# Counting pass of a graph kernel: a block's sums in one PSUM bank, the count as a column of each part, fewer vector operations

## What is computed

```python
h = jnp.maximum(_layernorm(x, axis=-1), 0.0)
x = x + _L1_gnn_ref(h, edge_index, L1_gnn_weight, L1_gnn_bias)

def _L1_gnn_ref(vertices, edges, weight, bias):
    ...
    agg = jax.ops.segment_sum(vertices[src], dst, num_segments=n_vertices)
    deg = jax.ops.segment_sum(jnp.ones_like(dst, dtype=vertices.dtype), dst, num_segments=n_vertices)
    agg = agg * (jnp.clip(deg, 1.0, None) ** (-0.5))[:, None]
    return agg @ weight.T + bias
```

## Time and profile before

| | |
|---|---|
| median of 3 runs | 6257.87 us (6255.64 to 6283.21) |
| the profiled execution's own time | 6250.27 us |
| its span | 6248.4 us |
| busy share of the span: PE, DVE, ACT, POOL | 76%, 77%, 58%, 21% |
| the counting pass in the trace | 2793.74 to 3337.51 us from the span's start |

### The profile page before, as it was taken

One profiled execution on the slowest core, in us unless ns is written; L12 is line 12 of the kernel. 1 busy time (PEld: TensorE's weight loads), 2 busy tenths in 40 slices (PEclk: granted clock), 3 DMA queues, 4 the chain that ended last, 5 costly groups with the idle time before them and its releaser, 6 DMA issues.

```text
span 6248.4 us, 250046 instructions
## 1 busy us (share of the span) xinstructions
PE 4754.4 (76%) x92226; PEld 3865.2 (62%) x92226; DVE 4828.7 (77%) x10876; ACT 3637.7 (58%) x10975; POOL 1301.5 (21%) x1884
## 2 busy tenths in 40 slices
PE   2566666663777777747775999996999997999997
PEld 1344444442666666636665999994666665666665
DVE  8999999998999999998887555556666665666665
ACT  3566666661333333336665666665777776777776
POOL 2555555553333333310000000000000000000000
PEclk7777777776778878869997999998999998999999
DMA  1000000002666666620001333332333332333332
GB/s 42 1 1 1 1 1 1 1 1 73 202 202 200 203 200 204 201 84 0 0 0 33 101 99 100 100 93 67 84 85 85 84 84 78 85 84 84 84 85 76
DMA packets 305213, 501.25 MB, mean 80 GB/s; under 512 B 76918, under 2 KB 78454, under 8 KB 305126
## 3 DMA queue, kind: packets, MB, share of 16 engines
q1 hardware_dynamic: 303782, 499.39, 27.8%
q0 software_dynamic: 576, 0.52, 0.0%
q10 hardware_dynamic: 768, 0.16, 0.0%
HBM read 408.40 MB, written 91.57 MB: 80 GB/s over the span
## 4 chain that ended last, share of the span: by engine, by line
issue 51%; DVE 25%; PE 14%; POOL 6%; DVEq 2%; DMA 1%; ACT 1%; POOLq 0%; ACTq 0%; SPq 0%
PE PS L1173 9%; DVE agg L1620 7%; POOL arena L627 5%; DVE arena L1584 5%; PE PS L1135 4%; DVE Hp L1584 3%; DVE arena L1626 2%; DVE tmp L1584 2%; PE PS L1180 1%; DVE arena L2161 0%; DVE arena L2171 0%; DVEq L1590 0%; DVE agg L2166 0%; DMA rows_h<-Hn 0%; DVE arena L1593 0%
## 5 line engine op out<-in xcount | busy, mean ns | idle before, releaser
L1584 DVE TENSOR_TENSOR arena<-iotab,arena 128x1024 bf16<-128x1024 bf16 (+6 forms) x1813 | 1760.4, 991 | 535.3 <-PE PS L1298 479.9
L910 ACT ACTIVATE arena<-PS 128x384 bf16<-128x384 f32 x2450 | 1076.9, 491 | 519.3 <-PE PS L1291 507.4
L1298 PE MATMUL PS<-arena 32*128 32x192 bf16 x41552 | 1069.7, 243 | 1.7 <-ACT arena L910 1.1
L748 ACT ACTIVATE arena<-PS,m 128x196 bf16<-128x196 f32 x1813 | 743.8, 429 | 547.1 <-POOLq L527 328.7
L1298 PEld LDWEIGHTS PS<-arena 32*128 32x128 bf16 x41552 | 806.2, 93 | 181.8 <-issue 156.5
L1135 PE MATMUL PS<-Hp,arena 128*128 128x72 bf16 (+1 forms) x14700 | 809.0, 204 | 104.8 <-DVE arena L1950 41.1
L1135 PEld LDWEIGHTS PS<-Hp,arena 128*128 128x128 bf16 x14700 | 696.8, 102 | 132.2 <-DVE arena L1950 41.3
L1291 PE MATMUL PS<-Hp,arena 128*128 128x192 bf16 (+1 forms) x4900 | 664.5, 250 | 115.8 <-DMA arena<-hots 60.0
L1023 PE MATMUL PS<-arena,tmp 128*128 128x262 bf16 x1813 | 508.9, 329 | 290.0 <-DVE tmp L1584 289.6
L891 ACT ACTIVATE arena<-PS,ewB 128x64 f32<-128x64 f32 x2450 | 534.8, 332 | 291.4 <-PE PS L1135 291.3
L1015 PE MATMUL PS<-agg,onesb 128*128 128x196 bf16 x1715 | 516.8, 303 | 202.5 <-ACT arena L748 198.1
(11 more groups left out here) (351 smaller groups left out, 7782.7 us busy)
## 6 DMA issues: line engine op xcount, KB each, us to landing
arena<-hots SPq DMA_DIRECT2D x735, 256.0 KB, 2.6
arena<-codes SPq DMA_DIRECT2D x245, 512.0 KB, 4.2
hots<-arena SPq DMA_DIRECT2D x245, 256.0 KB, 4.2
arena<-hots SPq DMA_DIRECT2D x147, 320.0 KB, 2.9
arena<-codes SPq DMA_DIRECT2D x49, 640.0 KB, 4.4
hots<-arena SPq DMA_DIRECT2D x49, 320.0 KB, 4.5
rows_h<-Hn SPq DMA_DIRECT2D x4, 1568.0 KB, 9.1
rows_l<-Y SPq DMA_DIRECT2D x1, 1764.0 KB, 10.4
```

The lines of the kernel that those rows point to most:

```text
L748: act.activation(junk[:, j % 4, :], ps[j % 4][:, 0:KEYS], ACT.Relu, bias=m256[:, 0:1], accum_out=rank[:, j:j + 1]).then_inc(k_rank, 1)
L910: act.activation(RG[g % 2][:, 2 * i:2 * i + 2, :].rearrange("p k c -> p (k c)"), ps[q % 2][:, 0:2 * RW], ACT.Copy).then_inc(r_ev, 1)
L1298: last = pe.matmul(ps[2 + q][:, b * RW:(b + 1) * RW], one_hot[32 * q:32 * q + 32, b * P:(b + 1) * P], rows_of[32 * q:32 * q + 32, :], star ...
L1584: return dve.tensor_tensor(to.rearrange("p k (n t) -> p k n t", t=4), iota_of[:, 0:n].rearrange("p (n t) -> p n t", t=4)[:, None, :, :] .t ...
```

## The change

`Hp` and the few's values get three parts of 65 columns each in this pass: 64 features and a count column, which is one in the first part and zero in the other two (`CV` = 65, `CW` = 195). All groups and the few of a block accumulate in bank 6. `evict` runs once a block, after group 1 of the next block: one reduction over the three parts of 65 columns, then one addition to the 65 columns of `agg`. The bank is given back between the two. `few` compares all three columns in one operation, from the fp32 `iota`, where there were three from the bf16 `iotab`. On DVE two more short memsets of `Hp` stand ahead of the pass, on POOL one more of the few's values.

```diff
-        CW = PARTS * DIM + 1
+        CW = PARTS * CV
...
-                mlink(pool.memset(c_W3m[:, :, 3 * DIM:CW], 1.0))
+                mlink(pool.memset(c_W3m, 0.0))
+                mlink(pool.memset(c_W3m[:, :, DIM:CV], 1.0))
...
-                    act.activation(Hp[:, ws, DIM:2 * DIM], Hn[:, ws, :], ACT.Copy).then_inc(s_h1, 1)
+                    act.activation(Hp[:, ws, v:v + DIM], Hn[:, ws, :], ACT.Copy).then_inc(s_h1, 1)
...
-                h = g // 3
-                to = ps[6 + h][:, 0:CW]
+                to = ps[6][:, 0:CW]
                 pe.wait_ge(f_whole, n + (NN + 3))
-                if g % 3 == 0:
-                    pe.wait_ge(f_accout, dx * 2 + (2 * WINDOWS + h + 1))
+                if g == 0:
+                    pe.wait_ge(f_accout, dx * 2 + (2 * WINDOWS + 2))
...
-            dve.memset(Hp[:, :, 3 * DIM:CW], 1.0)
+            for a in range(PARTS):
+                dve.memset(Hp[:, :, a * CV + DIM:(a + 1) * CV], float(a == 0))
...
-                def evict(dx, h):
-                    if h == 0:
-                        dve.wait_ge(f_scat, dx * NG + (NN + 3 + 3))
-                    else:
-                        dve.wait_ge(f_sum, dx + (WINDOWS + 1))
-                    got = ps[6 + h]
-                    flink(dve.tensor_reduce(c_part[:, 0:DIM], got[:, 0:RW].rearrange("p (a c) -> p c a", a=PARTS),
-                                            AX.X, ALU.add))
-                    to = agg[:, bass.ds(dx, 1), 0:DIM].rearrange("p w c -> p (w c)")
-                    degree = agg[:, bass.ds(dx, 1), DIM:DIM + 1].rearrange("p w c -> p (w c)")
-                    flink(dve.tensor_tensor(degree, degree, got[:, RW:CW], ALU.add))
-                    flink(dve.tensor_tensor(to, to, c_part[:, 0:DIM], ALU.add))
-                    dve.sem_inc(f_accout, 1)
+                def evict(dx):
+                    dve.wait_ge(f_sum, dx + (WINDOWS + 1))
+                    flink(dve.tensor_reduce(c_part, ps[6][:, 0:CW].rearrange("p (a c) -> p c a", a=PARTS), AX.X, ALU.add))
+                    dve.sem_inc(f_accout, 2)
+                    to = agg[:, bass.ds(dx, 1), 0:CV].rearrange("p w c -> p (w c)")
+                    flink(dve.tensor_tensor(to, to, c_part, ALU.add))
...
-                    for m in range(MC):
-                        last = dve.tensor_scalar(c_OM[:, m, :], iotab[:, 0:P],
-                                                 msrel[:, bass.ds(dx, 1), m:m + 1].rearrange("p w c -> p (w c)"), None,
-                                                 ALU.is_equal)
-                    last.then_inc(f_ohm, 1)
+                    dve.tensor_tensor(c_OM, iota[:, 0:P][:, None, :].to_broadcast((P, MC, P)),
+                                      bc(msrel[:, bass.ds(dx, 1), :].rearrange("p w c -> p (w c)"), P),
+                                      ALU.is_equal).then_inc(f_ohm, 1)
...
-                        if g == 2 and not first:
-                            evict(dx - 1, 1)
+                        if g == 1 and not first:
+                            evict(dx - 1)
                         if g == 3:
                             few(dx)
-                        if g == 5:
-                            evict(dx, 0)
```

More of the change, by code:

```diff
@@ L267, in gnn_stack @@
         c_OM = cv.take(MC * P, bf16).rearrange("p (m n) -> p m n", m=MC)
-        c_part = cv.take(WIDE)
+        CV = DIM + 1
+        c_part = cv.take(CV)
         c_Gm = cv.take(MC * DIM).rearrange("p (m c) -> p m c", m=MC)
         c_Rm = cv.take(MC * DIM).rearrange("p (m c) -> p m c", m=MC)
-        CW = PARTS * DIM + 1
+        CW = PARTS * CV
         c_W3m = cv.take(MC * CW, bf16).rearrange("p (m c) -> p m c", m=MC)
@@ L665, in _ @@
                 gather_few(c_Gm, th[1], 1)
-                mlink(pool.memset(c_W3m[:, :, 3 * DIM:CW], 1.0))
+                mlink(pool.memset(c_W3m, 0.0))
+                mlink(pool.memset(c_W3m[:, :, DIM:CV], 1.0))
                 pool.wait_ge(f_mg, 16 * 3 * MC)
-                split_few(c_Gm, c_Rm, c_W3m, DIM, DIM, 2 * DIM, 0)
+                split_few(c_Gm, c_Rm, c_W3m, DIM, CV, 2 * CV, 0)
             pool.wait_ge(s_table, 16 * 4)
@@ L714, in squares_and_roots, with parts_of_h @@
                                    scale=1.0 / DIM).then_inc(s_std, 1)
-            def parts_of_h(n):
+            def parts_of_h(n, v=DIM):
                 for h, ws in enumerate(HALVES):
                     act.wait_ge(s_h, 2 * n + h + 1)
-                    act.activation(Hp[:, ws, DIM:2 * DIM], Hn[:, ws, :], ACT.Copy).then_inc(s_h1, 1)
+                    act.activation(Hp[:, ws, v:v + DIM], Hn[:, ws, :], ACT.Copy).then_inc(s_h1, 1)
                 for h, ws in enumerate(HALVES):
                     act.wait_ge(s_hrest, 2 * n + h + 1)
-                    act.activation(Hp[:, ws, 2 * DIM:3 * DIM], tmp[:, ws, :], ACT.Copy).then_inc(s_h2, 1)
+                    act.activation(Hp[:, ws, 2 * v:2 * v + DIM], tmp[:, ws, :], ACT.Copy).then_inc(s_h2, 1)
             def copy_turned(n):
@@ L837, in _ @@
             squares_and_roots(2)
-            parts_of_h(1)
+            parts_of_h(1, CV)
             act.wait_ge(s_begin, 2)
@@ L1230, in apply @@
                         Hp[:, bass.ds(dx, 1), 0:CW].rearrange("p w c -> p (w c)")
-                    last = pe.matmul(to, AB[g % 3][:, k * P:(k + 1) * P], rhs, start=(g % 3 == 0 and k == 0),
-                                     stop=(g == 2 and k == GS[g] - 1))
+                    last = pe.matmul(to, AB[g % 3][:, k * P:(k + 1) * P], rhs, start=(g == 0 and k == 0), stop=False)
                 last.then_inc(f_scat, 1)
@@ L1425, in _, with split_h @@
             hs = [0]
-            def split_h():
+            def split_h(v=DIM):
                 n = hs[0]
@@ L1431, in split_h @@
                     dve.wait_ge(s_h1, 2 * n + h + 1)
-                    dve.tensor_tensor(tmp[:, ws, :], Hn[:, ws, :], Hp[:, ws, DIM:2 * DIM],
+                    dve.tensor_tensor(tmp[:, ws, :], Hn[:, ws, :], Hp[:, ws, v:v + DIM],
                                       ALU.subtract).then_inc(s_hrest, 1)
@@ L1435, in split_h, with norm_relu @@
                     dve.wait_ge(s_h2, 2 * n + h + 1)
-                    dve.tensor_tensor(Hp[:, ws, 0:DIM], tmp[:, ws, :], Hp[:, ws, 2 * DIM:3 * DIM],
+                    dve.tensor_tensor(Hp[:, ws, 0:DIM], tmp[:, ws, :], Hp[:, ws, 2 * v:2 * v + DIM],
                                       ALU.subtract).then_inc(s_hparts, 1)
-            def norm_relu(v):
+            def norm_relu(v, width=DIM):
                 center(v)
@@ L1443, in norm_relu @@
                                              op0=ALU.max, op1=ALU.mult).then_inc(s_h, 1)
-                split_h()
+                split_h(width)
             def copy_y(n):
@@ L2114, in _ @@
             OFS = [0]
-            for links in (5, 6, 3, 2, 2):
+            for links in (5, 2, 3, 2, 2):
                 OFS.append(OFS[-1] + links * WINDOWS)
@@ L2135, in _ @@
             link(dve.tensor_tensor(X[:, :, :], X[:, :, :], tmp[:, :, :], ALU.add))
-            norm_relu(X[:, :, :])
+            norm_relu(X[:, :, :], CV)
             dve.sem_inc(s_th, 1)
-            dve.memset(Hp[:, :, 3 * DIM:CW], 1.0)
+            for a in range(PARTS):
+                dve.memset(Hp[:, :, a * CV + DIM:(a + 1) * CV], float(a == 0))
             dve.tensor_copy(wide, Hn[:, :, :])
@@ L2188, in count_pass @@
                 with dve.Fori(1, WINDOWS) as d:
-                    at[0], at[1] = d * 6 + (ofs - 3), 0
+                    at[0], at[1] = d * 2 + (ofs - 2), 0
                     body(d, False)
-                at[0], at[1] = ofs + 6 * WINDOWS - 3, 0
-                evict(LASTW, 1)
+                at[0], at[1] = ofs + 2 * WINDOWS - 2, 0
+                evict(LASTW)
             with dve.If(runs > 1):
```

## The result

The median went from 6264.6 us (four runs of the kernel before, 6255.6 to 6283.2) to 6179.4 us (four runs, 6174.4 to 6187.2); ratio 0.986, interval 0.983 to 0.989. The profiled execution of the changed kernel took 6187.2 us with a span of 6185.2. The difference of the medians is 85 us, that of the two profiled executions 63 us; both need an account.

What follows compares the result with a forecast made beforehand. DVE was taken to set the counting pass's pace. Gains of 1.8 + 59.3 − 0.3 − 0.2 = 60.6 us took the profiled 6250.3 to 6189.7; 7.6 more for the median gave 6197 us, range 6180 to 6217.

Steps and rivals of the forecast that it cites:

- the sum: Counting pass and the memsets ahead: 1.8 + 59.3 − 0.3 − 0.2 = 60.6 us gained.
- the last step: From profiled execution to median: 6189.7 us plus 7.6, the runs' median being above the profiled execution, so 6197.
- The period: One block of the counting pass on DVE: 9.69 us, 1.29 less than 10.98.
- The low clock: Short clock drops in the counting pass: kept at their old price, 4 us; gone, they would give 4 back.
- more is gained: Rival: no low clock (4 us), a cheaper few's operation (12 us), or either: 6181 to 6193; chance 0.17.
- The ends: First and last block of the counting pass: 1.8 us gained at the start, 0.3 lost at the end.
- the loop's turn: At a block's end on DVE: 0.30 us, taken as hidden behind two comparisons without a wait between.
- the new wait: DVE ahead of the remaining evict's reduction, waiting for PE's sums: 0.63 us a block.
- the single bank: At apply(0) of the new block: bank back at 3.85 us against 3.84 before, costing PE nothing at full clock.
- the few's operation: The few's one-hots on DVE: one operation at 0.48 us against three at 0.49, so nothing gained.
- PE is just in time: PE ahead of build(0): of 1.74 us idle the removed evict takes 1.63, leaving 0.11.
- The slower rival: New waits at the single bank break up PE's bursts, the clock drops; at half the pass 6312 us; chance 0.03.

Runs made afterwards that it cites:

- e1: The changed kernel again, no edit, beside the kernel before: median 6185.1 us against 6284.7, ratio 0.983.
- e2: The changed kernel with the few's one-hots made by three operations again: 6189.0 us, ratio 0.986 to the kernel before.
- e4: The kernel before once more, no edit, a single profiled execution: counting pass 542.2 us, time 6259.0 us.
- e3: The changed kernel with the one evict behind group 2 of the next block instead of group 1: median 6173.1 us, ratio 0.981.
- e9: The changed kernel with the one evict behind group 0 instead of group 1: counting pass 559.1 us, single execution 6271.7 us.
- e11: The changed kernel plus an unread vector addition of 2176 elements in group 5, pausing PE 2.43 us: pass 621.6 us, execution 6334.9 us.
- e8: The changed kernel plus an unread vector addition of 1408 elements in group 5, pausing PE 1.62 us: counting pass 546.1 us.
- e10: The changed kernel with the one evict behind group 3 instead of group 1: counting pass 443.2 us, single execution 6145.7 us.
- e12: The changed kernel with the evict behind group 3, timed in six runs: median 6157.7 us, ratio 0.986 to the kernel before.
- e5: The changed kernel plus 167 extra unread matmuls ahead of the weight pass: median 6176.1 us, ratio 0.9882 to the kernel before.
- e7: The changed kernel with the evict behind group 2 and 167 extra matmuls ahead of the weight pass: 6148.4 us, ratio 0.9839.

## Why the prediction was wrong, point by point

The mechanism of the counting pass was right, and two terms of the time were not. The forecast was 6197.3 and the median 6179.4, 17.9 us less. Of these, 10.2 are the sum, 60.6 us where the pass gave 70.8, and 7.6 are the last step: "the median of the runs is 7.6 above it, so 6197". That distance was no property of the kernel: the median of the changed kernel's runs lay 7.8 *below* its profiled execution, and that of the kernel before rose from 6257.9 to 6264.6 with one more run. Either error alone would have left the result inside the range. The profiled execution, forecast at 6189.7 and measured at 6187.2, was nearly met by luck: the pass gave 10.2 us more, and the stages around it took 7.6 more (by chance the same figure).

The range was built from bounds of the pass alone and held nothing for the rest of the kernel, where single executions differ by ten us and at times by 40 to 70. The prediction had a sign of that before it and read it wrongly: "in the pass behind this one PE is never idle and the clock is 1.00 throughout" holds for the stretch in the earlier trace rows, but from 3398 to 3426, at the start of that same pass, the clock was 0.50:

```profile
3398.00:3415.00 17.00, 13.25 (x138) 0.50 0.43 123
3415.00:3426.00 11.00, 11.00 (x107) 0.50 0.18 49
```

It is this low start, 29 us long here, that reached 120 us in e1 and about 185 in e2. What it does to the times of single executions:

| trace | counting pass | weight pass | time |
|---|---|---|---|
| before | 543.8 | 798.9 | 6250.3 |
| e4, before again | 542.2 | 799.9 | 6259.0 |
| changed | 473.0 | 799.4 | 6187.2 |
| e1, changed again | 473.2 | 842.0 | 6229.6 |
| e2 | 473.8 | 872.9 | 6260.2 |
| e3 | 445.9 | 843.2 | 6203.1 |

The weight pass accounts for the whole of what e1 has over the changed kernel's trace (42.6 us of 42.4) and for e2's (73.5 of 73.0). The runs beside the traces, those of the first comparison too, have no trace of their own, so that their differences come from there isn't shown.

The terms of the sum, 60.6 where the pass gave 70.8:

- *The period*, 9.69, measured 9.57: 47 times 0.12 is 5.4 us. The sums came at 3.31 us of the block, as reckoned (3010.97 less the block's first comparison, which is four comparisons, 2.41 us, behind 3005.25, at 3007.66). The error is the evict, taken at 1.08 and measured at 0.97 (0.12 us idle behind the addition, not 0.31; the two comparisons ahead of it end later by what one operation overlaps the next, which is why the wait reads 0.55 and not 0.63), and 0.01 in the few.
- *The low clock*, "I take them at their old price": all falls went, and 4.0 us with them. This was the rival "more is gained" in its first half. PE's gap of 1.74 us is gone with them; e9 and e11 show that gaps of 2.4 us bring falls back, and e8 leaves open whether 1.74 alone would.
- *The ends*: 0.3 more at the start, 0.2 at the end; the memsets' 0.2 lie ahead of the pass and not in it.

Together 10.1 of the 10.2.

What held: DVE bounds the pass; the loop's turn is hidden; the new wait exists; the single bank costs the pass nothing (e3 and e10: not even when it comes back 0.6 and 1.8 us later in the block); the few's operation is worth under 1 us (e2); the odd columns of `Hp` cost nothing (its writes again take 3.49 to 3.50 us a pair). The prediction's "PE is just in time" held too: of the 0.11 us reckoned 0.09 is there.

The slower rival did not occur in the changed kernel, but the danger is real: e9 is the changed kernel with the evict 1.2 us earlier on DVE, and its pass is 15 us longer than before the change.

Left open: why the weight pass stays at the lower clock for 29 to about 185 us of its start while PE is busy, and whether the change alters how often. On the two chips with many long runs (those of e1 to e4 and of e12), 14 of 22 runs of the kernel before and 8 of 25 runs of changed kernels lay 15 us or more above the lowest of their kind on that chip. That would make the medians differ by more than the pass, as they did in e1, but it is a count and no cause. Busy PE ahead of the pass (e5 to e7) improves the start by some 10 us in the traces and does not exclude the long runs.

## What to carry to other kernels

Where two engines hand each other blocks, reckon a moved wait from both sides: when the result can be there at the earliest, and when the waiting engine arrives. Moving the evict by one pair of comparisons (0.55 us of waiting a block, 27 us in all) was worth nearly two fifths of what the change itself gave, and the same move the other way lost all of it (e9, one execution). A second buffer isn't needed where the one comes back inside the slack of its writer; look at the writer's idle time before paying for it (here PE waited 0.63 and 1.06 us a block for the bank and the pass lost nothing). And a range for a whole kernel must hold the spread of the stages that the change doesn't touch: take it from several executions, and compare stages in the traces where medians disagree.

## What was not expected of the hardware

- The granted clock of TensorE falls for a third of a 10 us stretch at a time (0.83), in most blocks when PE is idle 2.4 us in one piece in a block of 10.8 to 11.9 us (e9, e11), in four to six of 49 blocks of the kernel before, with 1.74 us, and never with 1.62 (e8). At 2.4 it costs the pass of e11 some 36 us: 621.6 us for 49 blocks, of which an undisturbed one takes 11.91 (e8, undisturbed, has 546.1 for 49 blocks of 11.11, 1.7 over).
- In the weight pass the clock stayed at the lower level for up to about 185 us from the pass's start, with PE busy without a break from 3350 on (e2: 0.50 from 3331 to 3500, 0.84 in the next 50 us), at a cost of 73 us against the changed kernel's first trace, and rose by itself. Some 70% of the time of the pass's matmuls is fp32; whether that matters wasn't tried.
